# A transformer block on one core: the prologue in another order, the spline factors spread over attention periods, and all periods written out

## The chip, the core and the metric

One NeuronCore of a Trainium2 chip runs the whole program. The metric is the device time of one execution in microseconds (us). TensorE (PE) does matmuls and transposes, VectorE (DVE), ScalarE (ACT) and GpSimd (POOL) the rest; SyncE (SP) and, here also ScalarE, issue DMAs.

## What is computed

For x of 16 blocks of 256 tokens by 256 channels in float32, four residual steps follow one another (cut from the reference):

```python
x = x + attn_a(layernorm(x), Wq, Wk, Wv, Wo)        # 16 heads of 16, causal softmax
x = x + ffn(layernorm(x), gate_cp, up_cp, down_cp)
x = x + attn_b(layernorm(x), Wq, Wk, Wog, Wig, g_weight)  # gated linear attention, 16 keys
x = x + ffn(layernorm(x), gate_cp, up_cp, down_cp)

def ffn(h):
    gate_w, up_w, down_w = (spline_reconstruct(cp) for cp in ...)   # cubic, 2033 points to 1024 x 256
    return (silu(h @ gate_w.T) * (h @ up_w.T)) @ down_w.T
```

## The kernel before

Each engine has its own instruction list, written by hand; engines meet at semaphores only. The lists run through five stages: a prologue, the softmax attention, the first FFN, the gated attention (GLA), the second FFN.

Attention takes the 16 blocks one after the other in `period(b, j, u)`, with eight steps `p` (a step is a pair of heads from each half of the array). In step p TensorE computes for block b the scores with the row maxima subtracted (`shifted`, L878), for block b+1 the plain scores whose row maxima VectorE takes (`scores` L847, `hide_future` L859, `maxima` L1703), and every second step it weighs the values (`weigh`, L892 and L896). ScalarE takes the exponential (`exps`, L1322) and POOL zeroes what lies ahead of the diagonal (`mask`, L668). Between these stand the transposes and projections of block b+2 (`turn_x` L818, `proj_qk` with the three-matmul product `mm3` L414 to L416) and the end of block b-1 (`turn_o` L905, `turn_att` L913, `proj_out`). Q and K in high and low float parts are staged in `stage` (L1310, L1694) and moved by DMA into `stack` (L505), whose partitions hold the parts that one matmul contracts; six DMAs of 128 KB make one half of the stack (`stack_half`), two halves a block. Four small DMAs a half bring the maxima as rows (`max_rows`, L513). `run_periods` writes out periods 0, 1 and 12 to 15 and runs 2 to 11 as a loop of two.

The prologue, before period 0: SP loads the first X (L481), eight weights in a row on one semaphore (L483, L485), further X and the spline tables. VectorE sets constant rows of `stack` with four memsets (L1646) and then normalises block 0. TensorE waits for all eight weights, transposes them into `prep_bank` (L805, L809), ScalarE and VectorE split each in a high and a low part, and then come blocks 0 and 1 up to their stack rows, and the scores of block 0.

The weights of the FFN come from spline control points as low-rank factors. POOL makes them in `factors(w)` for gate, up and down (L678 product, L681, L683 and L686 sums) and `low_factors` (L690), before `rstd(2, 0)` and the first mask. In period 0 TensorE transposes the factors (`turn_factors` L934, one of four in each of steps 0 to 3; `turn_down` L945 in steps 6 and 7), ScalarE stores them (L1344, L1349). In period 1 `down_rows` (L959, K = 42) and `spread_rows` (L1360, L1362) make the down weight, which SP stores to DRAM at the end of period 1, together with two DMAs of zero rows.

Of the kernel before, what the change touches and what calls it, by code (L numbers as in the profile page):

```python
# [26 lines left out]
P = 128  # L27
B = 16
# [120 lines left out]
def build(nc, x, a_wq, a_wk, a_wv, a_wo, b_wq, b_wk, b_wog, b_wig, g_weight, cpw_in, psi_in, feat_in, mom_in,  # L149
          starts, out):  # L150
    outer = ExitStack()
    with outer:
# [14 lines left out]
        prep_bank = bank + [pair_a[:, 0], pair_a[:, 1], pair_b[:, 0], pair_b[:, 1]]  # L167
        fill_bank = prep_bank[2:] + prep_bank[0:2]
# [116 lines left out]
        s_w = sem("weights_loaded")  # L285
# [9 lines left out]
        s_stack = sem("stack_rows_set")  # L295
# [175 lines left out]

        def out_bank(u, q):

            return ((bank_o, bank_y)[q][:, :], pair_b[:, q, :])[1 - u]
# [5 lines left out]
        def _(sp):  # L480
            sp.dma_start(X[:, 0:TB, :], x_t[:, 0:TB, :]).then_inc(s_x[0], 16)  # L481
            for n, w in enumerate((a_wq, a_wk, a_wv, a_wo, b_wog, b_wig)):
                sp.dma_start(wnat[:, n], w.rearrange("(o p) c -> p o c", p=P)).then_inc(s_w, 16)  # L483
            for n, w in enumerate((b_wq, b_wk)):
                sp.dma_start(bnat[:, n, :], w).then_inc(s_w, 16)  # L485
            sp.dma_start(X[:, TB:2 * TB, :], x_t[:, TB:2 * TB, :]).then_inc(s_x[1], 16)
            sp.dma_start(cpw[:, :, :, :].rearrange("p w m k -> p (w m k)"), cpw_in).then_inc(s_cp, 16)
            sp.dma_start(flat[:, 14 * D:14 * D + MT * NF * WIN], psi_in).then_inc(s_cp, 16)
            sp.dma_start(X[:, 2 * TB:4 * TB, :], x_t[:, 2 * TB:4 * TB, :]).then_inc(s_x[2], 16)
            lead(sp, a_stk + a_md + f_.sp)  # L490
            sp.dma_start(mom[:, :, :], mom_in).then_inc(s_mom, 16)

            def stack_half(b, u, h, after_use=True):
# [4 lines left out]
                if after_use:  # L498
                    sp.wait_ge(a_stp, upto(a_stp, b - 2, 4 * h + 4))
                for a in range(2):  # L500
                    src = slice(HALF * a, HALF * a + HALF)
                    for r in range(3):
                        rows = slice(HALF * a + DK * r, HALF * a + DK * r + DK)
                        slots = slice(2 * r, 2 * r + 2) if r < 2 else slice(0, 4, 3)
                        sp.dma_start(stack[rows, u, h].bitcast(F32),  # L505
                                     stage[src, h, slots, :].bitcast(F32)).then_inc(a_stk[h], 16)

            def max_rows(b, u, h):
                sp.wait_ge(a_ml, upto(a_ml, b, h + 1))
                for a in range(2):  # L510
                    for n in range(2):
                        row = HALF * a + K_S + n
                        sp.dma_start(stack[row:row + 1, u, h, :, 0, :].bitcast(F32),  # L513
                                     mrow[PR * a:PR * a + PR, h, n, :].bitcast(F32)).then_inc(a_md[h], 16)

            for b in range(2):
                for h in range(2):
                    if not h:
                        sp.wait_ge(s_stack, 2 * b + 2)
                    if b and h:  # L520
                        max_rows(0, 0, 0)
                    stack_half(b, b, h, False)
            sp.wait_ge(s_c, 12)
            sp.dma_start(feat.rearrange("p r c -> p (r c)"), feat_in).then_inc(s_feat, 16)
# [12 lines left out]
            def period(b, j, u, prev=True, nxt=True, nxt2=True, nxt3=True):  # L537
                if not isinstance(b, int) or b < B - 4:
# [11 lines left out]
                if isinstance(b, int) and b == 1:  # L550
                    store_down()
                    sp.wait_ge(s_zero, 1)
                    for half in range(2):
                        sp.dma_start(copies[half, :, D, :].rearrange("v (p k) -> v p k", k=32),
                                     zeros[48 * half:48 * half + 48, :]).then_inc(s_zeros, 16)
# [83 lines left out]
        def _(pool):  # L639
# [3 lines left out]
                               pattern=[[-1, P]], channel_multiplier=1).then_inc(s_ident, 1)  # L643
            lead(pool, by_pool + f_.pool + g_.pool)
            pool.memset(causal_neg[:, :, :, :], 0.0).then_inc(s_const, 1)
            pool.memset(half_neg[:, :], -0.5).then_inc(s_const, 1)
            pool.memset(quarter[:, :], 0.25).then_inc(s_const, 1)
            pool.memset(V[:, :, :, :, DK:DK + 1], 1.0).then_inc(s_const, 1)
            pool.memset(V[:, :, :, :, DK + 1:32], 0.0).then_inc(s_const, 1)
            pool.wait_ge(s_const, 5)  # L650
            for n in range(2):
                i = pool.affine_select(out=causal_neg[:, n], in_=causal_neg[:, n], compare_op=ALU.is_ge,
                                       fill=NEG, base=HALF * n, pattern=[[-HALF, 2], [1, P]],
                                       channel_multiplier=-1)
            i.then_inc(s_const, 1)
            pool.wait_ge(s_ident, 2)
            pool.tensor_copy(ident16[:, :], ident[:, :]).then_inc(s_const, 1)
# [1423 lines left out]
```

## Time and profile before

| | us |
|---|---|
| median of three runs (lowest, highest) | 851.18 (848.19, 854.52) |
| the profiled execution, device time | 852.93 |
| its span, first to last instruction | 851.2 |
| mean granted TensorE clock | 0.962 |
| PE, DVE, ACT, POOL busy | 776.4, 629.5, 494.8, 237.0 |

The span lies 1.7 us under the device time. Busy times are sums over the span; a share says nothing of the stage that it falls in, so the readings below go by stages. L12 is line 12 of the kernel.

### The profile page before, as it was taken

The page shows a single profiled execution, that of the slowest core. Times are in us where ns is not written, and L with a number is a line of the kernel's source. Part 1 is how long each engine was busy: PE and PEld are TensorE (multiplying, and loading weights), DVE is VectorE, ACT ScalarE, POOL GpSimd, SP SyncE. Part 2 cuts the span into 40 slices and gives each one's busy share as a digit, 9 for nine tenths or more (in the row PEclk, how much of TensorE's full clock was granted, in tenths as well). Part 3 has the DMA queues.
Part 4 walks back from the last instruction along what each step waited for, and adds up shares of the span by engine and source line. Part 5 has one row for each costly group of instructions (what it writes and reads, how often), then busy time and mean ns, then how long its engine had stood idle before and what let it go on. Part 6 is the DMA issues. An engine that isn't in the chain of part 4 may idle for free.

```text
span 851.2 us, 19705 instructions
## 1 busy us (share of the span) xinstructions
PE 776.4 (91%) x6676; PEld 657.4 (77%) x6676; DVE 629.5 (74%) x1272; ACT 494.8 (58%) x967; POOL 237.0 (28%) x306
## 2 busy tenths in 40 slices
PE   3689999999999999977999989999998879999988
PEld 3567767777777777746988889888888758889887
DVE  7464777777777788836778777789989748887765
ACT  3135545455454555655666657588878746666653
POOL 2942222223232223321000010055656552000000
PEclk9767999999999999977999999999999989999999
DMA  5946566666666654577565651000034125777741
GB/s 183 112 69 88 94 124 100 88 88 88 98 98 94 96 80 78 109 248 262 204 230 218 255 204 45 1 2 2 2 111 168 42 79 202 255 259 272 267 159 50
DMA packets 70960, 111.16 MB, mean 131 GB/s; under 512 B 7061, under 2 KB 27958, under 8 KB 70854
## 3 DMA queue, kind: packets, MB, share of 16 engines
q1 hardware_dynamic: 70896, 110.35, 51.0%
q8 instruction: 35, 0.57, 0.3%
q14 instruction: 29, 0.24, 0.1%
HBM read 41.82 MB, written 42.81 MB: 99 GB/s over the span
## 4 chain that ended last, share of the span: by engine, by line
PE 51%; DVE 14%; issue 9%; DMA 8%; SPq 8%; ACT 6%; POOL 3%; ACTq 0%; DVEq 0%; POOLq 0%
PE bank L414 8%; PE bank L415 6%; PE bank L416 6%; DMA stk<-fx 5%; PE pair_a L878 4%; SPq L586 4%; PE bank L892 4%; PE pair_b L847 4%; DVE inter L1874 3%; DMA fx<-fs 3%; PE pair_a L1166 2%; ACT gact L1457 2%; DVE spline L1952 2%; PE bank L1201 2%; DVE spline L1961 1%
## 5 line engine op out<-in xcount | busy, mean ns | idle before, releaser
L414 PE MATMUL bank<-wd_hi,in_hi 128*128 128x256 f32 x512 | 145.5, 284 | 1.4 <-DVE in_lo L1879 0.9
L416 PE MATMUL bank<-wd_hi,in_lo 128*128 128x256 f32 x512 | 144.9, 283 | 0.0
L415 PE MATMUL bank<-wd_lo,in_hi 128*128 128x256 f32 x512 | 144.5, 282 | 0.0
L668 POOL TENSOR_SCALAR_AFFINE_SELECT prob<-prob 128x512 f32<-128x512 f32 x128 | 82.1, 642 | 217.3 <-ACT prob L1322 217.3
L1322 ACT ACTIVATE prob<-pair_a 128x768 f32<-128x768 f32 x128 | 103.7, 810 | 66.5 <-PE pair_a L878 65.5
L1465 ACT ACTIVATE in_hi<-inter 128x512 fp32r<-128x512 f32 x128 | 80.8, 631 | 105.7 <-DVE inter L1874 100.6
L1703 DVE TENSOR_REDUCE mx<-pair_b 128x6 f32<-128x768 f32 x124 | 118.0, 952 | 26.2 <-PE pair_b L859 25.3
L1879 DVE TENSOR_TENSOR in_lo<-inter,in_hi 128x512 fp32r<-128x512 f32 x128 | 89.1, 696 | 60.5 <-ACT in_hi L1465 59.0
L414 PEld LDWEIGHTS bank<-wd_hi,in_hi 128*128 128x128 f32 x512 | 96.7, 189 | 6.9 <-DVE in_lo L1879 1.7
L415 PEld LDWEIGHTS bank<-wd_lo,in_hi 128*128 128x128 f32 x512 | 96.5, 188 | 4.6
L416 PEld LDWEIGHTS bank<-wd_hi,in_lo 128*128 128x128 f32 x512 | 96.5, 189 | 0.0
L1874 DVE TENSOR_TENSOR inter<-gact,pair_b 128x512 f32<-128x512 f32 x128 | 87.1, 680 | 3.2 <-ACT gact L1457 2.2
L1457 ACT ACTIVATE gact<-pair_a 128x512 f32<-128x512 f32 x128 | 74.5, 582 | 3.3 <-PE pair_a L1111 3.3
L878 PE MATMUL pair_a<-stack 50*128 50x256 f32 x512 | 66.9, 339 | 10.2 <-ACT prob L1322 6.2
L878 PEld LDWEIGHTS pair_a<-stack 50*128 50x128 f32 x512 | 40.1, 191 | 36.1 <-issue 14.7
L847 PE MATMUL pair_b<-stack 48*128 48x256 f32 x496 | 57.0, 307 | 7.4 <-DVE stage L1694 3.7
L1111 PE MATMUL pair_a<-stk,cst 126*128 126x512 f32 x128 | 52.5, 410 | 9.4 <-DMA stk<-fx 8.1
L720 POOL TENSOR_TENSOR frs<-fve,half_neg 128x4 f32<-128x4 f32 x16 | 16.7, 1041 | 142.1 <-DVE fve L1853 142.1
L1114 PE MATMUL pair_b<-stk,cst 126*128 126x512 f32 x128 | 53.0, 414 | 1.7 <-DVE inter L1874 1.6
L1310 ACT ACTIVATE stage<-bank 128x512 fp32r<-128x512 f32 x32 | 19.2, 599 | 56.7 <-PE bank L416 52.0
L847 PEld LDWEIGHTS pair_b<-stack 48*128 48x128 f32 x496 | 40.0, 194 | 14.6 <-DVE mx L1703 7.6
L892 PE MATMUL bank<-prob,V 128*32 128x256 f32 x512 | 42.3, 403 | 0.3 <-POOL prob L668 0.2
(226 smaller groups left out, 1953.1 us busy)
## 6 DMA issues: line engine op xcount, KB each, us to landing
stk<-fx SPq DMA_DIRECT2D x128, 252.0 KB
stack<-stage SPq DMA_DIRECT2D x192, 128.0 KB, 4.7
fx<-fs SPq DMA_DIRECT2D x32, 512.0 KB, 3.4
fx<-fs SPq DMA_DIRECT2D x32, 256.0 KB, 3.6
fx<-fs SPq DMA_DIRECT2D x16, 504.0 KB
fx<-fs SPq DMA_DIRECT2D x16, 252.0 KB
X<-in_attn_a_x SPq DMA_DIRECT2D x14, 256.0 KB, 5.1
result<-X SPq DMA_DIRECT2D x7, 512.0 KB, 7.9
```

The costliest lines, as they stand in the source:

```text
L414: pe.matmul(dst, l_hi, r_hi, start=first, stop=False)
L415: pe.matmul(dst, l_hi, r_lo, start=False, stop=False)
L416: return pe.matmul(dst, l_lo, r_hi, start=False, stop=last)
L668: pool.affine_select(out=diag, in_=diag, compare_op=ALU.is_ge, fill=0.0, base=0, pattern=[[0, 2], [0, 2], [1, P]], channel_multiplier=-1). ...
L847: pe.matmul(dst[:, n, at_col:at_col + S], stack[rows, u, h, p % PR, 0, P * t:P * t + P], stack[rows, u, h, p % PR, 1, :], start=(t == 1), ...
L878: i = pe.matmul(pair_a[:, n, at_col:at_col + S], stack[rows, u, h, p % PR, 1, P * t:P * t + P], stack[rows, u, h, p % PR, 0, :], start=Tru ...
L1322: act.activation(prob[:, p % 4], pair_a[:, :, P:4 * P], ACT.Exp, scale=DK ** -0.5).then_inc(a_e, 1)
L1457: act.activation(gact[:, m % 2, :], pair_a[:, m % 2, :], ACT.Silu).then_inc(f_.si, 1)
L1465: act.activation(in_hi[:, m % LAG, :], inter[:, m % 2, :], ACT.Copy).then_inc(f_.ih, 1)
L1703: dve.tensor_reduce(mx[:, h, :, p % PR, :], src[:, :, 0:3 * P].rearrange("p n (t k) -> p n t k", t=3), AX.X, ALU.max).then_inc(a_mx, 1)
L1874: dve.tensor_tensor(inter[:, m % 2, :], gact[:, m % 2, :], pair_b[:, m % 2, :], ALU.mult).then_inc(f_.up, 1)
L1879: dve.tensor_tensor(in_lo[:, m % LAG, :], inter[:, m % 2, :], in_hi[:, m % LAG, :].bitcast(F32), ALU.subtract).then_inc(f_.il, 1)
```

## The change

1. Prologue. SP issues X of block 0, Wq, Wv, X of block 1, Wo, X of blocks 2 and 3; ScalarE issues Wk, Wog, Wig and the two small weights before its semaphore counts. Wq and Wk, and Wv, have semaphores of their own. VectorE keeps one memset of `stack` rows, POOL does the other three, and POOL's constants are ordered by need. TensorE takes the weights one by one, mixed with block 0 and 1; the second `proj_qk` of a block goes to another bank. Between them stand `keep_clock(n)`, n matmuls of 128 x 128 bf16 whose result nobody reads.
2. The spline tables are loaded behind the stack rows of blocks 0 and 1. Of each half, ScalarE issues the two DMAs of r = 2 and SP the four others.
3. The factors are 24 pieces on POOL (eight a weight), one behind each mask from step 4 of period 0 to step 3 of period 3; the low parts follow in steps 4 and 5 of period 3.
4. Two turns a period: `turn_factors` in periods 4 and 5, `turn_down` in 6, `down_rows` in 7 and 8, in steps 0 and 1, with two banks in turn. The store of the down weight follows period 8, the zero rows go one each to periods 1 and 2, the load of `feat` to period 3.
5. All periods are written out.
6. The DMAs of r < 2 name a row of 2 KB (`(k s)`) where they named two of 1 KB.

The core of the diff:

```diff
-            period(1, 0, 1)
-            with eng.Fori(1, B // 2 - 2) as j:
-                period(2 * j, j, 0)
-                period(2 * j + 1, j, 1)
-            period(B - 4, B // 2 - 2, 0)
+            for b in range(1, B - 3):
+                period(b, b // 2, b % 2)
...
+        def stack_rows(eng, u, h, r):
+            for a in range(2):
...
+                to, of = stack[rows, u, h].bitcast(F32), stage[src, h, slots, :].bitcast(F32)
+                if r < 2:
+                    to, of = to.rearrange("p i k s -> p i (k s)"), of.rearrange("p k s -> p (k s)")
+                eng.dma_start(to, of).then_inc(a_stk[h], 16)
...
             def period(b, j, u, prev=True, nxt=True, nxt2=True, nxt3=True):
                 for p in range(NP):
                     mask(b, p)
+                    if 4 <= NP * b + p < 28:
+                        factor_piece(NP * b + p - 4)
+                    if NP * b + p in (28, 29):
+                        low_factors(p - 4)
...
+            def keep_clock(n, dst=bank_y):
+                for _ in range(n):
+                    pe.matmul(dst[:, 0:P], ident16[:, :], ident16[:, :], start=True, stop=True)
...
+            pe.wait_ge(s_ident, 3)
+            keep_clock(40, pair_b[:, 1])
+            pe.wait_ge(s_wqk, 32)
+            turn_weight(0)
+            turn_weight(1)
+            turn_x(0, 0)
+            pe.wait_ge(s_wv, 16)
+            turn_weight(2)
+            keep_clock(8, pair_b[:, 1])
+            pe.wait_ge(s_prep_lo, 2)
+            pe.wait_ge(a_xl, upto(a_xl, 0, 1))
+            proj_qk(0, 0, 0)
+            proj_qk(0, 0, 1, bank_o)
+            pe.wait_ge(s_prep_lo, 3)
+            proj_v(0, 0)
+            turn_x(1, 1)
+            keep_clock(16, pair_b[:, 1])
+            turn_weight(3)
+            keep_clock(8, pair_b[:, 1])
+            pe.wait_ge(a_xl, upto(a_xl, 1, 1))
+            pe.wait_ge(a_qkl, upto(a_qkl, 0, 1))
+            proj_qk(1, 1, 0)
+            pe.wait_ge(s_const, 6)
+            pe.wait_ge(s_prep_lo, 4)
+            keep_clock(16)
+            for p in range(4):
+                hide_future(scores(0, 0, p, both=True))
+                if p == 1:
+                    keep_clock(8)
+            pe.wait_ge(a_qkl, upto(a_qkl, 0, 2))
+            proj_qk(1, 1, 1, bank_o)
+            turn_max(0, 0)
+            keep_clock(6)
+            for p in range(4, NP):
+                hide_future(scores(0, 0, p, both=True))
+                if p == 5:
+                    keep_clock(8)
+            for n in range(4, 6):
+                turn_weight(n)
+                keep_clock(16, bank_t)
...
+                    if 4 <= b < 9 and p < 2:
+                        if p == 0:
+                            pe.wait_ge(a_at, upto(a_at, b - 1, 1))
+                        else:
+                            pe.wait_ge(a_res, upto(a_res, b - 2, 1))
+                        if b < 6:
+                            turn_factors(2 * (b - 4) + p)
+                        elif b == 6:
+                            turn_down(p)
+                        else:
+                            down_rows(2 * (b - 7) + p)
+                    if 4 <= b < 9 and p in (2, 3):
+                        if b < 7:
+                            pe.wait_ge(s_ce, 2 * (b - 4) + p - 1)
+                        else:
+                            pe.wait_ge(s_wdn, 2 * (b - 7) + p - 1)
```

## Rows read from the trace of the kernel before

**Rows 1.** The page: TensorE's granted clock in tenths, 40 equal slices.

```profile
PEclk9767999999999999977999999999999989999999
```

**Rows 2.** Windows: start:end, length, busy us per engine, clock, DMA share, GB/s.

```profile
0.00:47.21 47.21, 23.96 (x170) 20.64 (x170) 29.48 (x54) 10.24 (x22) 29.76 (x31) 0.85 0.73 144
47.21:72.42 25.21, 22.48 (x220) 16.73 (x218) 15.75 (x35) 12.62 (x19) 7.07 (x11) 0.80 0.49 71
72.42:100.10 27.68, 27.36 (x263) 22.16 (x260) 15.68 (x33) 14.55 (x30) 6.05 (x9) 0.82 0.49 72
100.10:121.81 21.71, 19.68 (x234) 15.02 (x234) 15.86 (x34) 10.35 (x16) 5.81 (x9) 1.00 0.70 132
121.81:301.65 179.84, 175.12 (x2054) 134.19 (x2052) 139.16 (x289) 92.17 (x135) 52.34 (x81) 1.00 0.65 94
301.65:321.36 19.71, 19.26 (x232) 14.90 (x228) 15.53 (x33) 10.24 (x15) 5.82 (x9) 1.00 0.58 85
33.60:57.40 23.80, 18.16 (x130) 13.45 (x131) 15.59 (x27) 4.98 (x8) 16.13 (x14) 0.51 0.76 101
74.50:84.80 10.30, 10.30 (x71) 8.46 (x71) 2.74 (x4) 6.15 (x16) 1.28 (x2) 0.52 0.54 66
```

**Rows 3.** Timeline of the prologue: start us, length us, engine, line, out<-in [idle before, releaser].

```profile
2.37 1.28 ACT L1291 ACT_TABLE_LOAD   x1 [2.37 <-issue]
...
8.05 1.76 DVE L1646 MEMSET stack<- 32x2048 f32 x1 [0.48 <-issue]
...
9.84 0.75 DVE L1651 BATCH_NORM_STATS2 st<-X 128x6 f32<-128x256 f32 x2
...
10.49 3.64 PE L805 MATMUL bank<-ident,spline 128*128 128x128 f32 x16 [10.49 <-DMA spline<-in_attn_b_Wk]
...
18.39 0.39 PE L414 MATMUL bank<-xT_hi,wq_hi 128*128 128x256 f32 x1 [1.48 <-DVE xT_lo L1689]
...
21.77 14.19 SPq L505 DMA_DIRECT2D stack<-stage  x18
...
30.76 0.60 ACT L1310 ACTIVATE stage<-bank 128x512 fp32r<-128x512 f32 x1 [4.78 <-DMA stack<-stage]
...
32.13 0.50 PE L847 MATMUL pair_b<-stack 48*128 48x256 f32 x4 [3.69 <-DVE stage L1694]
...
33.68 0.95 DVE L1703 TENSOR_REDUCE mx<-pair_a 128x6 f32<-128x768 f32 x1
...
47.21 0.81 ACT L1322 ACTIVATE prob<-pair_a 128x768 f32<-128x768 f32 x1 [4.69 <-PE pair_a L878]
```

**Rows 4.** Timeline of POOL's factor work and the transpose behind it.

```profile
21.15 4.25 POOL L678 TENSOR_TENSOR spline<-spline,cpw 128x2016 f32<-128x2016 f32 x1 [3.23 <-DVE xn L1663]
...
28.38 1.09 POOL L686 TENSOR_TENSOR cx<-spline 128x336 f32<-128x336 f32 x1
...
47.76 0.71 PEld L934 LDWEIGHTS bank<-ident,cx 128*126 128x126 f32 x4 [0.20 <-POOL cx L690]
```

**Rows 5.** Timeline of one middle period: second mask, its weighing, four transposes.

```profile
184.47 0.64 POOL L668 TENSOR_SCALAR_AFFINE_SELECT prob<-prob 128x512 f32<-128x512 f32 x1 [1.07 <-ACT prob L1322]
...
185.48 0.64 PE L892 MATMUL bank<-prob,V 128*32 128x256 f32 x8
...
186.76 0.60 PE L905 MATMUL bank<-ident,oT 128*128 128x128 f32 x4
...
187.29 0.50 PE L878 MATMUL pair_a<-stack 50*128 50x256 f32 x4
```

**Rows 6.** Timeline of the down rows in period 1: matmuls and their ScalarE copies.

```profile
77.52 2.87 PE L959 MATMUL bank<-spline 42*128 42x128 f32 x12
...
79.58 0.84 ACT L1360 ACTIVATE spline<-bank 128x192 f32<-128x192 f32 x2 [0.76 <-PE bank L959]
...
80.22 0.36 ACT L1362 ACTIVATE spline<-bank 128x128 f32<-128x128 f32 x1
```

**Rows 7.** DMA totals of two stretches: 24 to 34 us, then 168 to 188 us.

```profile
DMA packets 962, 1.26 MB, mean 126 GB/s; under 512 B 151, under 2 KB 546, under 8 KB 962
...
q1 hardware_dynamic: 962, 1.26, 109.2%
...
DMA packets 1564, 1.88 MB, mean 94 GB/s; under 512 B 240, under 2 KB 1052, under 8 KB 1564
```

More of the change, by code:

```diff
@@ L497, in stack_half @@
                 sp.sem_inc(passed_sp, 1)
[L498 to L506, printed above, removed]
+                sp.wait_ge(a_stp, upto(a_stp, b - 2, 4 * h + 4))
+                for r in range(3):
+                    stack_rows(sp, u, h, r)
             def max_rows(b, u, h):
@@ L549, in period @@
                     stack_half(b + 2, u, 1)
-                if isinstance(b, int) and b == 1:
+                if b in (1, 2):
+                    sp.wait_ge(s_zero, 1)
+                    sp.dma_start(copies[b - 1, :, D, :].rearrange("v (p k) -> v p k", k=32),
+                                 zeros[48 * (b - 1):48 * b, :]).then_inc(s_zeros, 16)
+                if b == 3:
+                    sp.wait_ge(s_c, 24)
+                    sp.dma_start(feat.rearrange("p r c -> p (r c)"), feat_in).then_inc(s_feat, 16)
+                if b == 8:
                     store_down()
[L552 to L555, printed above, removed]
                 if nxt and not nxt2:
@@ L643, in _, with ones_rows @@
                                pattern=[[-1, P]], channel_multiplier=1).then_inc(s_ident, 1)
+            pool.wait_ge(s_ident, 2)
+            pool.tensor_copy(ident16[:, :], ident[:, :]).then_inc(s_ident, 1)
+            pool.memset(half_neg[:, :], -0.5).then_inc(s_const, 1)
             lead(pool, by_pool + f_.pool + g_.pool)
[L645 to L657, printed above, removed]
-            pool.memset(zeros[:, :], 0.0).then_inc(s_zero, 1)
+            def ones_rows(u, a):
+                rows = slice(HALF * a + 2 * DK, HALF * a + HALF)
+                pool.memset(stack[rows, u, :, :, 1].bitcast(F32), 1.0).then_inc(s_stack, 1)
+                pool.wait_ge(s_stack, 2 * u + a)
             def rstd(b, u):
@@ L691, in low_factors @@
                                    ALU.subtract).then_inc(s_c, 1)
+            pool.wait_ge(s_const, 1)
+            ones_rows(0, 1)
             rstd(0, 0)
+            pool.memset(quarter[:, :], 0.25).then_inc(s_const, 1)
+            pool.memset(V[:, :, :, :, DK:DK + 1], 1.0).then_inc(s_const, 1)
+            pool.memset(V[:, :, :, :, DK + 1:32], 0.0).then_inc(s_const, 1)
             rstd(1, 1)
-            pool.wait_ge(a_xn, upto(a_xn, 1, 2))
-            for w in range(3):
-                factors(w)
-            for w in range(2):
-                low_factors(w)
+            pool.memset(causal_neg[:, :, :, :], 0.0).then_inc(s_const, 1)
+            pool.wait_ge(s_const, 5)
+            for n in range(2):
+                i = pool.affine_select(out=causal_neg[:, n], in_=causal_neg[:, n], compare_op=ALU.is_ge,
+                                       fill=NEG, base=HALF * n, pattern=[[-HALF, 2], [1, P]],
+                                       channel_multiplier=-1)
+            i.then_inc(s_const, 1)
+            pool.wait_ge(s_const, 6)
+            ones_rows(1, 0)
+            ones_rows(1, 1)
             rstd(2, 0)
-            pool.wait_ge(s_prep_lo, 7)
+            pool.memset(zeros[:, :], 0.0).then_inc(s_zero, 1)
             def period(b, j, u, prev=True, nxt=True, nxt2=True, nxt3=True):
@@ L1641, in _ @@
         def _(dve):
-            for u in range(2):
-                for a in range(2):
-                    rows = slice(HALF * a + 2 * DK, HALF * a + HALF)
-                    dve.memset(stack[rows, u, :, :, 1].bitcast(F32), 1.0).then_inc(s_stack, 1)
+            dve.memset(stack[2 * DK:HALF, 0, :, :, 1].bitcast(F32), 1.0).then_inc(s_ones, 1)
             lead(dve, by_dve + f_.dve + g_.dve)
@@ L1777, in period @@
                         maxima(b + 1, p)
+                        if b == 0 and p == 1:
+                            low_gla_weights()
                         if p == 3:
```

334 lines of the change are left out of this document (172 added, 162 removed).

## The prediction

> **What bounds the kernel now.** I read four views in this order. The page's clock line [rows 1] first: TensorE is granted less than its full clock in two places, at the start and near slices 18 and 19. Then the windows from the first exponential of one attention period to the next [rows 2], which give the length of each piece of the attention stage; the reader should see that nine periods in the middle take 179.84 us (19.98 each) with TensorE busy 175.12 us at clock 1.00, so they are bound by TensorE, while the prologue takes 47.21 us with TensorE busy 23.96, and the first three periods take 25.21, 27.68 and 21.71 us. Against a middle period that is 14.9 us too much in the three. Third, the timeline of the prologue [rows 3] and its POOL and TensorE rows [rows 4], to see what arrives late. Fourth, the timeline of one middle period [rows 5], because the work that leaves the prologue goes there.
>
> The prologue is a queue of late starts. VectorE sets constant rows until 9.81 us and only then reads the first X [rows 3]. TensorE waits for the last of eight weight loads and starts its transposes at 10.49. The first projection runs at 18.39, the first stack loads are issued at 21.77, the copy of the next projection waits for them until 30.76, and the first scores run at 32.13. From there to the first exponential at 47.21 are 15.1 us, of which the eight row maxima take 8 x 0.95; the clock is 0.51 in 33.6 to 57.4 [rows 2]. Beside that chain POOL makes the spline factors from 21.15 on, and TensorE's first factor transpose, at 47.76, waits for the last of them [rows 4]. So two chains end within a microsecond, and taking away the POOL one alone would give little.
>
> **The change, part by part.** The sum is made against the profiled execution, 852.93 us, which lies 1.75 above the median of 851.18.
>
> *Earlier start of the prologue.* Three of the four VectorE memsets go to POOL or behind other work, so the statistics need only X and one memset (1.76 us from about 1.3, then some 1 to 2 us of semaphore counts): about 4 us instead of 9.84. The weights are issued on two queues, and TensorE waits for Wq and Wk alone. ScalarE now issues five loads ahead of its semaphore counts and table load, which began at 2.37 and take 1.28 [rows 3]; at some 0.5 us an issue it is ready at about 6.5. Then one weight eviction pair, xn, its transpose, and the two halves of xT give the first projection at about 9.8 (18.39 before, 8.6 earlier). From projection to stack issue stays 3.4, so the stack loads begin at about 13.
>
> *Stack loads.* A half of the stack is six loads of 128 KB. In 24 to 34 us the DMA engines are full at 1.26 MB in 10 us [rows 7], which makes 6.2 us a half. First issue to the wait's end was 9.0 us. Two of six issues go to ScalarE, some 1.3 us less of serial issue on SP, so I take 7.8 us: half 0 lands at about 20.9, and half 1, behind it, by 26. The rearranged rows of r < 2 ask for 2 KB pieces, but a middle period's 1564 packets hold 512 of 2 KB or more [rows 7], which is exactly eight loads of 64: these rows are 2 KB already. I cost that edit at nothing. Were they 1 KB after all, the two thirds of each half that they carry could at most move in half their time, 2 us off the wait for a half; the other bound is 0. The Trainium skill, "DMA: Bandwidth & Descriptors", section "Issuing engines are not separate DMA queues", says that issuing from several engines saves only the issue time, because all share 16 engines; by it the ScalarE issues give the 1.3 us and no more, whereas a second stream of its own would land half 0 some 3 us sooner. The full share in [rows 7] sides with the rule.
>
> *From the first scores to period 0.* Scores start at 20.9. VectorE then has eight maxima (7.6) and the evictions, merges and splits between them: of the 15.1 us before, 7.5 were not maxima, and I take 4.2 for these at full clock, together 11.8, with the wait for half 1 inside. TensorE has, after its last scores, two weight transposes (0.53 per four at full clock, [rows 5]; twice that cold) and 32 filler matmuls, 2 to 4 us. I take 13.6 us to the first exponential, 15.1 before, so 34.5. Gain 12.7 us. Bounds: 9 (the path from 32.13 is as long as before and the clock low) to 17 (the tail of weight transposes hidden).
>
> *Periods 0 to 2.* Factor and down-row work leaves them, and the clock, if kept, is 1.00. Period 0: a middle period less the part of the previous block (output projection, three groups of four transposes, a weighing), 17.5 us, gain 7.7. Period 1: 20.1, gain 7.6. Period 2: 20.0, gain 1.7; it was long because SP issued the 1 MB store and the zero rows between stack loads and max rows (its DMA rate is 132 GB/s against 94). Zero rows stay in 1 and 2, half each: at most 0.5 us each.
>
> *Written-out periods.* The one written-out period with the same work takes 19.71 [rows 2], the looped ones 19.98. Nine of them: minus 2.4 us. Lower bound of the gain 0, if the difference belongs to what is late in that period.
>
> *POOL pieces.* The factor work, 8.3 us a weight (21.15 to 29.47), is cut in eight pieces of at most 1.09 us ([rows 4]: 4.25 over four, and 1.09), one behind each mask in slots 4 to 27. What is queued behind a piece on POOL is the next mask, and behind that the weighing on TensorE. In a middle period the second mask starts at 184.47 and ends at 185.11; its weighing starts at 185.48 [rows 5]. The mask before ends 1.07 us ahead of it ([rows 5], the idle time). A piece makes the second mask at most 0.2 late, against a slack of 0.37. Cost 0, up to 0.4 a period for three periods. POOL also waits for the factor tables, which SP now issues behind all stack rows of both blocks, at about 33; with 1.2 MB behind the last half they land at about 42, and the piece comes at about 43. No wait, or up to 3 us if both err.
>
> *Turns in periods 4 to 8.* These periods are TensorE-bound, so this lies on the path. Six groups of four transposes at 0.53 [rows 5] make 3.2 us. The down rows are 32 matmuls, twelve of them in 2.87 us at clock 0.5 [rows 6], 0.22 each with what overlaps, so 0.11 at clock 1.00: 3.5 us (bound 7.0). ScalarE sits between them: a store is an eviction of 0.60, as the copy in [rows 3], and down rows are 0.84 + 0.36 [rows 6], and it stands between two exponentials, for which TensorE's next step waits. I take 0.5 us of stall in the three lighter periods and 1.0 in the two heavier ones, 3.5 in all (bounds 0 and the whole ScalarE work, 9). The 1 MB store now follows period 8: 1.2 us, as period 2 shows its like. Together 11.3.
>
> *Rest.* FFN and GLA stages are the same. Sum: -12.7 - 7.7 - 7.6 - 1.7 - 2.4 + 11.3 = -20.8, so 832.1 for the profiled execution and 830.4 by the median.
>
> **The rivals.** (a) The clock is lost as before, after the prologue and once more in periods 4 to 8. It fell at 33.6, after TensorE had stood idle for 3.69 us ahead of the first scores [rows 3], and again in 74.5 to 84.8, while the down rows ran [rows 2]. A stretch of 10.3 us at half clock can cost TensorE-bound work 5.1 us and work that waits for others nothing; I take 4.5, since the middle periods are TensorE-bound. Two of them: 839. For: maxima on VectorE pace TensorE at less than half busy. Against: fillers stand at those gaps. The Trainium skill, "TensorE: Matmul & The Clock Gate", Part 4, says that transposes do not count as activity for the clock; a prologue full of transposes would then start cold. The trace has 16 transposes from 10.49 [rows 3] and no loss behind them: a mean of 0.85 over the prologue [rows 2] is what half clock from 33.6 alone gives; I give the rule part of this rival's chance, and its cost here would be the transposes at twice their time, some 3 us. (b) The added turns are absorbed by TensorE's small gaps and ScalarE never stalls, and the tail of the prologue is hidden: 830.4 - 3.5 - 4 = 823. (c) Slower side: masks become the bound. If each piece came ahead of a mask that TensorE waits for, all 24 pieces and the two low parts, at 1.06 on average ([rows 4]: 4.25 over four), would be on the path, 27.5 us, and the time 858. It decides once a piece, mask and handover exceed the 1.71 us between the first masks by more than 0.37, in every slot; the mean spacing of masks is 19.98 / 8 = 2.5 us, which speaks against it. (d) The new order does not start sooner because X, Wq and Wk land late beside other loads and ScalarE's table load comes last: the first projection at 14 instead of 9.8, result 835.
>
> **How the numbers follow.** My forecast has 0.55, (a) 0.18, (b) 0.12, (d) 0.12, (c) 0.03. The likeliest gives 830.5. The range 821 to 841 takes in (a), (b) and (d) with the bounds of the stall and the prologue tail. About 1% (8.5 us) is what a measurement of this kernel can tell from no change; only (c), or a sum of (a) and (d) with another lost stretch, reaches that: faster by over 1% 0.93, within 1% 0.05, slower 0.02.
>
> **What would show it.** First projection at about 10, first scores at 21, first exponential at 34 to 35; period 0 near 17.5; periods 1 to 3 near 20 with clock 1.00; periods 4 to 6 at 21.2 and 7 and 8 at 22.5; unchanged packets of 2 KB a period; weighings that never name POOL as releaser. It would be wrong if the clock is low after 35 us, if scores wait for half 1 well after 26, or if the middle periods with pieces are longer than those without.

## The result, and the profile after

The changed kernel takes 841.9 us (median of 20 runs, 836.74 to 848.79) where the kernel before takes 850.63 (20 runs, 844.65 to 857.96): a ratio of 0.991, 95% interval 0.989 to 0.993. That is 8.7 us less, where 20.7 were forecast, and it lies just outside the forecast range of 821 to 841. The profiled execution took 838.48 us, its span is 836.7, and its mean granted clock 0.975.

The page's clock line first. A stretch in which TensorE is granted half its clock is called a lost stretch below. The low slices of [rows 1] near the start are gone but for one.

```profile
PEclk9899999999999999978999999999999999999999
```

The windows of the changed kernel, as in [rows 2]: the prologue, periods 0, 1 and 2, the nine periods 3 to 11, the six periods 4 to 9, period 8 alone, and all behind the last block's first exponential.

```profile
0.00:39.39 39.39, 29.24 (x308) 26.59 (x308) 23.73 (x47) 8.62 (x14) 10.92 (x21) 0.91 0.72 144
39.39:59.33 19.94, 16.58 (x200) 12.52 (x196) 15.45 (x38) 9.83 (x18) 10.24 (x13) 1.00 0.64 131
59.33:79.35 20.02, 19.45 (x230) 14.75 (x226) 16.37 (x34) 10.87 (x18) 14.78 (x18) 1.00 0.67 99
79.35:99.27 19.92, 19.50 (x232) 15.16 (x232) 16.39 (x33) 10.61 (x16) 14.07 (x17) 1.00 0.56 92
99.27:288.09 188.82, 179.96 (x2112) 140.51 (x2108) 140.45 (x291) 98.83 (x154) 57.75 (x88) 0.99 0.63 98
119.39:248.39 129.00, 122.04 (x1428) 95.83 (x1424) 93.04 (x193) 68.01 (x109) 34.75 (x54) 0.99 0.63 100
204.06:226.87 22.81, 22.25 (x248) 17.53 (x244) 15.34 (x32) 12.07 (x23) 5.79 (x9) 0.93 0.57 79
346.04:836.70 490.66, 451.33 (x3084) 405.68 (x3082) 366.55 (x730) 320.51 (x695) 117.42 (x137) 0.97 0.43 155
```

Against the profiled execution of before, stage by stage from the first exponentials:

| stage | forecast | measured |
|---|---|---|
| prologue | -12.7 | 39.39 - 47.21 = -7.8 |
| period 0 | -7.7 | 19.94 - 25.21 = -5.3 |
| period 1 | -7.6 | 20.02 - 27.68 = -7.7 |
| period 2 | -1.7 | 19.92 - 21.71 = -1.8 |
| periods 3 to 11 | -2.4 + 11.3 = +8.9 | 188.82 - 179.84 = +9.0 |
| all behind | 0 | -0.9 |
| sum | -20.8 | -14.5 |

The likeliest value forecast for the median was 830.5, and 841.9 was measured, 11.4 more (the remaining 0.6 of the 12.0 is the kernel before, whose median was 851.18 in three runs and 850.63 in twenty). Of these 11.4 us, 6.4 stand in this table, in its first two lines; the other 5.0 lie between the profiled execution and the median.

The prologue, as in [rows 3].

```profile
11.05 0.36 PE L416 MATMUL bank<-xT_hi,wq_hi 128*128 128x256 f32 x1 [0.94 <-DVE xT_lo L1770]
...
13.38 1.37 ACTq L484 DMA_DIRECT2D stack<-stage  x2
...
13.58 1.15 DVE L1744 TENSOR_SCALAR xn<-X,mv,rs 128x256 f32<-128x256 f32 x2 [0.82 <-POOL rs L676]
...
14.65 1.47 DVE L1775 TENSOR_TENSOR stage<-bank,stage 128x512 fp32r<-128x512 f32 x2
...
15.43 0.73 SPq L484 DMA_DIRECT2D stack<-stage  x1
...
24.68 0.80 PE L891 MATMUL pair_b<-stack 48*128 48x256 f32 x4 [3.42 <-DMA stack<-stage]
...
39.39 0.81 ACT L1384 ACTIVATE prob<-pair_a 128x768 f32<-128x768 f32 x1 [0.73 <-PE pair_a L922]
```

The first projection came at 11.05 (18.39 before). ScalarE issued its two loads at 13.38, but the low part, from which SP's four are made, stood on VectorE behind the normalising of block 1 and was done only for an issue at 15.43. The half landed for scores at 24.68, 9.3 us after SP's first issue and 11.3 after ScalarE's, with the DMA engines full: 18 to 28 us moved

```profile
DMA packets 871, 1.21 MB, mean 121 GB/s; under 512 B 145, under 2 KB 414, under 8 KB 871
```

against 1.26 MB in ten microseconds in [rows 7]. From there to the first exponential are 14.7 us, 15.1 before. This execution was a quick one here: in nine profiled executions with this prologue (seven of them with a change further on) the first exponential stands at 39.39 to 42.25 us, and 39.39 is the earliest.

The chain of work that ends period 0 (start, us, what):

```profile
53.91 0.23 PE bank L910 x2
54.16 0.42 DVE mrow L1797
54.61 0.42 DVE mrow L1799
55.05 0.67 SPq L489
55.76 0.65 SPq L489
56.45 0.57 SPq L489
57.06 1.69 DMA stack<-mrow
58.79 0.50 PE pair_a L922 x4
```

The reader should see the queue: the max of block 1 is transposed, split in two, issued by SP in four DMAs one after the other, and carried in 1.69 us; only then can TensorE start period 1. It stood 1.62 us for it, of 3.4 in all in a period in which it was busy 16.58 us; the other stops are under 0.6 each. In a middle period the same chain takes as long, 262.84 to 267.9, but the work of the block before fills the time. This is read from the trace; no run shortens the chain.

The timeline of period 4, then of period 9.

```profile
121.13 0.60 ACT L1406 ACTIVATE cst<-bank 126x512 fp32r<-126x512 f32 x1 [0.93 <-PE bank L974]
...
121.79 1.64 SPq L573 DMA_DIRECT2D spline<-down_features  x1
...
122.10 0.82 ACT L1384 ACTIVATE prob<-pair_a 128x768 f32<-128x768 f32 x1
...
123.94 1.34 SPq L489 DMA_DIRECT2D stack<-mrow  x2
...
130.12 0.50 PE L922 MATMUL pair_a<-stack 50*128 50x256 f32 x4 [1.34 <-DMA stack<-mrow]
...
229.27 0.61 SPq L544 DMA_DIRECT2D wdx<-spline  x1
...
231.07 3.15 SPq L489 DMA_DIRECT2D stack<-mrow  x4
...
237.26 0.50 PE L922 MATMUL pair_a<-stack 50*128 50x256 f32 x4 [1.78 <-DMA stack<-mrow]
```

The feature loads and the 1 MB store stand on SP ahead of the max rows, which are issued behind them and land late: TensorE stops 1.34 and 1.78 us in front of the second half of the block.

### The profile page after: what moved, and what is told of

Same layout as the page of the kernel before. It is cut to its first block, busy times and chain, and to the rows that moved or that the text cites. A ratio compares the mean times of both kernels' runs of the same rounds, so it can differ in the third digit from the quotient of the medians.

```text
span 836.7 us, 19306 instructions
## 1 busy us (share of the span) xinstructions
PE 772.9 (92%) x6818; PEld 658.4 (79%) x6818; DVE 626.0 (75%) x1269; ACT 493.8 (59%) x967; POOL 243.5 (29%) x321
## 2 busy tenths in 40 slices
DMA packets 70983, 111.48 MB, mean 133 GB/s; under 512 B 7061, under 2 KB 27958, under 8 KB 70854
## 4 chain that ended last, share of the span: by engine, by line
PE 54%; DVE 14%; issue 9%; SPq 8%; DMA 8%; ACT 7%; ACTq 0%; DVEq 0%; POOL 0%; POOLq 0%
PE bank L416 9%; PE bank L418 8%; PE bank L417 8%; PE pair_a L922 4%; DMA stk<-fx 4%; PE bank L936 3%; DVE inter L1961 3%; PE pair_b L891 3%; SPq L606 3%; SPq L489 3%; PE pair_a L1222 2%; PE pair_a L1167 2%; DMA stack<-mrow 2%; PE pair_b L1170 2%; DVE spline L2039 2%
## 5 line engine op out<-in xcount | busy, mean ns | idle before, releaser
L1784 DVE TENSOR_REDUCE mx<-pair_b 128x6 f32<-128x768 f32 x124 | 118.0, 951 | 35.0 <-PE pair_b L903 34.6
L417 PEld LDWEIGHTS bank<-wd_lo,in_hi 128*128 128x128 f32 x512 | 98.2, 192 | 4.8
L418 PEld LDWEIGHTS bank<-wd_hi,in_lo 128*128 128x128 f32 x512 | 98.2, 192 | 0.0
L922 PEld LDWEIGHTS pair_a<-stack 50*128 50x128 f32 x512 | 39.3, 188 | 39.6 <-DMA stack<-mrow 13.4
L891 PE MATMUL pair_b<-stack 48*128 48x256 f32 x496 | 54.6, 296 | 4.7 <-DMA stack<-stage 3.4
L1170 PE MATMUL pair_b<-stk,cst 126*128 126x512 f32 x128 | 54.9, 429 | 1.7 <-DVE inter L1961 1.6
```

Source lines behind the costliest of these rows:

```text
L417: pe.matmul(dst, l_hi, r_lo, start=False, stop=False)
L418: return pe.matmul(dst, l_lo, r_hi, start=False, stop=last)
L891: pe.matmul(dst[:, n, at_col:at_col + S], stack[rows, u, h, p % PR, 0, P * t:P * t + P], stack[rows, u, h, p % PR, 1, :], start=(t == 1), ...
L922: i = pe.matmul(pair_a[:, n, at_col:at_col + S], stack[rows, u, h, p % PR, 1, P * t:P * t + P], stack[rows, u, h, p % PR, 0, :], start=Tru ...
L1784: dve.tensor_reduce(mx[:, h, :, p % PR, :], src[:, :, 0:3 * P].rearrange("p n (t k) -> p n t k", t=3), AX.X, ALU.max).then_inc(a_mx, 1)
```

## The experiments

Unless said otherwise each changes the changed kernel. "Six periods" are 4 to 9, which hold all the moved turns and the store. The kernel before, run beside them, took 848.89 (first four), 850.38 (next four) and 851.09 us (last four).

**Before, written out.** The loop of before is replaced by its periods; nothing else.

```diff
-            with eng.Fori(1, B // 2 - 2) as j:
-                period(2 * j, j, 0)
-                period(2 * j + 1, j, 1)
+            for b in range(1, B - 3):
+                period(b, b // 2, b % 2)
```

> The kernel before with its ten looped attention periods written out, nothing else. Theory A (the loop costs 0.27 us a period, as the one written-out period of the same work showed): 2.7 us faster, ratio 0.997, each period 19.7. Theory B (the 0.27 belongs to what that one period leaves out; written-out code gives nothing back or has to be fetched): ratio 1.000 or above, periods at 20.0 or more. Theory B, if true, would account for part of the gain that is missing from the median.

Measured 846.49 us (12 runs), ratio 0.996 (0.993 to 0.999). Windows of period 1 and of the nine:

```profile
71.25:94.18 22.93, 22.61 (x262) 18.28 (x259) 15.56 (x33) 14.10 (x30) 6.06 (x9) 1.00 0.58 88
115.61:294.29 178.68, 173.28 (x2056) 134.05 (x2052) 138.68 (x289) 92.42 (x136) 52.34 (x81) 1.00 0.64 96
```

Five of the nine periods are 19.65, the others up to 20.60, and the nine are 1.2 us shorter than in [rows 2], the medians 2.4: the theory that the loop costs something stands, with 1 to 3 us. The row of period 1 says more. The work is that of before, with the down rows in it, and it takes 22.93 us at full clock where the profile of before has 27.68 at 0.82 [rows 2]. So 4.8 of the 7.6 us that I expected from period 1 belonged to a lost stretch, which the same work need not have.

**Turns twice.** TensorE's added matmuls of periods 4 to 8 are issued twice, ScalarE's copies once.

```diff
-                for k in range(4):
+                for k in (0, 1, 2, 3) * 2:
```

(the same in the three turn functions)

> The changed kernel with each group of factor transposes and down-row matmuls on TensorE done twice over. Theory A (this work lies on the path at full clock in periods 4 to 8): 6.7 us more than the changed kernel, ratio to the kernel before 0.999, periods 4 to 6 up by 1.1 and 7 and 8 by 1.8. Theory B (what makes periods 4 to 8 long is ScalarE's copies and the loads in between, TensorE has room): under 2 us more, ratio 0.992 to 0.993.

Measured 843.12 us (12 runs), ratio 0.992 (0.989 to 0.996). The window of the six periods, and behind it that of the next kernel, whose six periods are those of the changed kernel without the stretch of half clock in its period 8:

```profile
119.45:250.49 131.04, 126.34 (x1484) 101.02 (x1480) 93.06 (x193) 68.64 (x109) 34.88 (x54) 1.00 0.59 98
```

```profile
37.88:62.03 24.15, 20.66 (x200) 15.58 (x196) 16.83 (x40) 10.05 (x19) 10.32 (x13) 0.78 0.57 116
123.36:250.95 127.59, 120.52 (x1428) 94.90 (x1424) 93.06 (x193) 68.03 (x109) 34.74 (x54) 1.00 0.65 101
```

56 matmuls more cost 131.04 - 127.59 = 3.5 us, not the 6.7 that I had charged for the first 56. TensorE has some room there, but the work is not free. By the medians the two kernels cannot be told apart.

**No fillers.** The matmuls that are there only for the clock are left out.

```diff
-                for _ in range(n):
+                for _ in range(0):
                     pe.matmul(dst[:, 0:P], ident16[:, :], ident16[:, :], start=True, stop=True)
```

> The changed kernel without the 126 filler matmuls of the prologue. Theory A (they keep the clock up): clock low from about 24 us for 10 to 24 us, prologue and period 0 together 3 to 6 us longer, ratio to before 0.995 to 0.998. Theory B (the clock follows the idle stretch of 3.4 us before the first scores, which no filler covers, and TensorE is not the bound of the prologue): the same low stretch as with them, prologue shorter by the 3 us that the fillers take near its end, ratio 0.988 to 0.991.

Measured 844.58 us (12 runs), ratio 0.994 (0.991 to 0.997). The first exponential is 1.5 us earlier (37.88), and period 0 is 4.2 longer at clock 0.78 (above), period 1 1.3 longer. By the ratios the fillers earn 2.4 us, with intervals that overlap. That they keep the clock in periods 0 and 1 is not shown: five profiles with these fillers have a lost stretch there too, one of them 23.00 us at 0.78 in period 0 (both moves, below).

**One queue.** All six loads of a half, and the max rows, are issued by SP.

```diff
-                    for r in range(2):
+                    for r in range(3):
                         stack_rows(sp, b, h, r)
```

(with ScalarE's issues left out)

> The changed kernel with all stack and maximum rows of the prologue issued by SP, none by ScalarE. Theory A (the DMA engines are full from the first stack load on, so the queue that issues does not matter): first scores within 1 us of the 24.7 of the changed kernel, ratio to before 0.990 to 0.993. Theory B (issue time of 0.65 us each on SP sets the landing): first scores 1.3 to 2.6 us later, and again before period 0, ratio 0.994 to 0.996.

Measured 842.71 us (8 runs), ratio 0.990 (0.987 to 0.994), not to be told from the changed kernel.

```profile
16.46 7.81 SPq L484 DMA_DIRECT2D stack<-stage  x12
...
25.39 0.80 PE L889 MATMUL pair_b<-stack 48*128 48x256 f32 x4 [4.15 <-DMA stack<-stage]
```

The first scores come 0.7 us later than with two queues, but in this execution the first projection was 1.0 us later as well (12.08 against 11.05). From the first projection to the first scores are 13.3 us with one queue and 13.6 with two, so the 1.3 us of issue time that I had taken off were not to be had. The windows from the first issue to the landing, two queues and then one, show what else was moved:

```profile
13.38:24.68 11.30, 7.23 (x80) 6.67 (x78) 4.90 (x11) 2.29 (x4) 5.84 (x8) 0.98 0.85 116
```

```profile
16.46:25.39 8.93, 4.78 (x64) 4.54 (x62) 2.95 (x8) 1.68 (x3) 3.99 (x4) 0.88 0.88 117
```

The rate is the same. When half 0 had landed, 11.30 x 116 = 1.31 MB had moved with two queues and 8.93 x 117 = 1.04 MB with one, and half 0 is 0.79 MB of either. The loads of half 1 do not wait behind half 0, and ScalarE's two of them, issued at 15.43 beside SP's first, are the extra quarter of a megabyte.

**Stores behind the max rows.** Zero rows, feature loads and the 1 MB store are issued after the period's max rows.

```diff
                 max_rows(b, u, 1)
+                if b in (1, 2):
+                    sp.wait_ge(s_zero, 1)
...
+                if b == 4:
+                    sp.wait_ge(s_c, 24)
...
+                if b == 8:
+                    store_down()
                 if nxt2:
                     stack_half(b + 2, u, 0)
```

> The changed kernel with SP's large extra DMAs (zero rows in periods 1 and 2, the 336 KB of features, the 1 MB store) issued behind the first four maximum rows of a period, where the DMA engines are idle, instead of behind the last stack rows of a period. Theory A (they delay the maximum rows of the next period, for which TensorE waited 1.34 us in period 4): period 4 shorter by 1.2, period 9 by 1.5, periods 2 and 3 by 0.1, 3 us in all, ratio to before 0.987 to 0.988. Theory B (the DMA engines are short of time as a whole, and the delay only moves to the stack rows behind): periods 4, 8 and 9 together the same within 1 us, ratio 0.991.

Measured 836.12 us (5 runs, 834.42 to 838.66), ratio 0.984 (0.980 to 0.988).

```profile
119.89:243.95 124.06, 120.35 (x1428) 94.92 (x1424) 92.89 (x193) 67.85 (x109) 34.74 (x54) 1.00 0.65 104
```

The six periods lose 4.9 us against the changed kernel, or 3.5 against the one without a lost stretch: periods 4 and 9 fall from 21.88 to 20.58 and from 21.52 to 19.67, and both stops of TensorE are gone. Of the avoidable costs that were tried, this order was the largest.

**Later copies.** ScalarE's copies of the turned factors are put one step later.

```diff
-                    if 4 <= b < 9 and p < 2:
+                    if 4 <= b < 9 and 1 <= p < 3:
...
-                            store_factors(2 * (b - 4) + p)
+                            store_factors(2 * (b - 4) + p - 1)
```

> The changed kernel with ScalarE's copies of the turned factors and down rows one step later in its list, behind the next exponential, in periods 4 to 8. Theory A (periods 4 to 8 are long because the copy stands ahead of the next exponential, which TensorE waits for; doing TensorE's part twice cost only 2 us of 6.7): periods 4 to 8 shorter by 0.5 to 1 us each, 3 to 4 us in all, ratio to before 0.986 to 0.988. Theory B (TensorE's own added work sets the length): unchanged within 0.3 us a period, ratio 0.991.

Measured 838.8 us (5 runs), ratio 0.986 (0.982 to 0.990).

```profile
60.43:83.71 23.28, 23.13 (x230) 17.03 (x228) 15.69 (x33) 10.99 (x17) 14.58 (x17) 0.80 0.57 82
123.76:249.37 125.61, 120.42 (x1428) 95.08 (x1424) 92.82 (x193) 68.88 (x110) 34.88 (x54) 1.00 0.65 102
```

2.0 us less than 127.59 in the six periods: in the changed kernel the copy at 121.13 stood ahead of the exponential at 122.10. Periods 4 and 9, where TensorE stops for the max rows, stay at 21.8 and 21.5. Its period 1 shows the lost clock that the profile of the changed kernel has not, with the same program up to there.

**Whole factor operations.** 12 POOL operations of full size in place of the 24 pieces, in every second slot.

```diff
-                m = slice(2 * k, 2 * k + 2)
-                pool.tensor_tensor(prod[:, m], psi[:, m], ...
+                pool.tensor_tensor(prod, psi, ...
...
-                    if 4 <= NP * b + p < 28:
+                    if 4 <= NP * b + p < 28 and p % 2 == 0:
```

> The changed kernel with the factor work on POOL in 12 whole operations (4.25, 1.91, 0.8 and 1.1 us) behind every second mask of the same four periods, instead of 24 pieces of at most 1.1 us. Theory A (a late mask holds up the weighing on TensorE, and small pieces are what avoids it): each 4.25 us operation holds one mask up by about 2 us, periods 0 to 2 longer by 1 to 2.5 us each, ratio to before 0.994 to 0.998. Theory B (the weighing comes late enough, or the clock and VectorE hide it): within 0.5 us a period, ratio 0.991, and then the pieces of the change earn nothing over whole operations.

Measured 845.39 us (10 runs), ratio 0.994 (0.991 to 0.996), by the ratios 2.0 us more than with pieces. Period 2 is 21.23 us at full clock (19.92 in pieces). The timeline there:

```profile
97.60 4.24 POOL L694 TENSOR_TENSOR spline<-spline,cpw 128x2016 f32<-128x2016 f32 x1
...
98.92 2.94 DVE L1736 TENSOR_SCALAR ve<-mv 128x2 f32<-128x2 f32 x1
...
101.77 0.95 DVE L1782 TENSOR_REDUCE mx<-pair_b 128x6 f32<-128x768 f32 x1
...
102.77 0.50 PE L889 MATMUL pair_b<-stack 48*128 48x256 f32 x4 [1.06 <-DVE mx L1782]
```

I had expected late masks, and they are late. But the stop of TensorE names VectorE: an operation on 128x2 elements, 0.17 us elsewhere, lasts until POOL's product ends, and the maximum behind it is late by that. So the size came as expected, and part of the mechanism is another.

**Early low part.** Both moves, and the low part of block 0 ahead of the normalising of block 1.

```diff
-            normalise(1, 1)
             low_qk(0, 0)
+            normalise(1, 1)
```

> The changed kernel with both edits above, the large DMAs in the gap and the copies one step later, and VectorE's low part of the first projection ahead of the normalisation of block 1 in the prologue. Theory A for both: 6 us from them, and stack loads issued 1.1 us sooner, first exponential near 38.5 instead of 39.4; ratio to before 0.982 to 0.985. If only one of them holds: 0.986 to 0.988. Theory B for both: 0.990 to 0.991.

Measured 834.98 us (5 runs), ratio 0.982 (0.978 to 0.985).

```profile
15.37 5.44 SPq L484 DMA_DIRECT2D stack<-stage  x8
...
26.04 0.51 PE L891 MATMUL pair_b<-stack 48*128 48x256 f32 x4 [3.60 <-DMA stack<-stage]
```

In this execution X reached the transposed form 1.2 us later (11.41 against 10.22), so from there SP's issue is 1.3 us sooner, but the half took 10.7 us from it to land. From the first projection (12.24) to the first scores are 13.8 us, against 13.6 in the changed kernel, so the earlier issue buys nothing that can be seen. The first exponential came at 42.55, not at the 38.5 expected: a second lost stretch of 3.4 us, from 37.3, is in that time.

**Once more.** The changed kernel unchanged, profiled again.

> The changed kernel as it is, profiled a second time beside the next three kernels. Theory C (the profile of after that the prediction is held against was a quick execution, and typical ones lose the clock once more in periods 0 and 1): the profile shows either periods 0 and 1 of 19.9 to 20.1 us as before, or one of them at 22 to 23.5 us with a stretch of half clock of 3 to 10 us; median 840 to 843 on this chip. Rival (the clock never falls there in this kernel and the median lies above the profile for another reason, FFN and GLA stages): no stretch of half clock between 35 and 100 us, and the rest after the last block more than 2 us longer than the 490.7 of the first profile.

Measured 841.89 us (6 runs), ratio 0.989 (0.985 to 0.994); this profiled execution took 841.99, the median itself.

```profile
346.50:840.30 493.80, 451.95 (x3084) 406.25 (x3082) 366.87 (x730) 320.39 (x695) 117.52 (x137) 0.97 0.43 154
```

The attention stage agrees within 0.5 us, period by period within 0.12. The rest is 3.1 us longer. So the rival holds for this pair: it is in the FFN and GLA stages, which the change does not touch, that this typical execution is longer than the first one. Cut into four stretches of the same work, the rest takes 130.96, 24.00, 185.00 and 150.70 us in the first execution at clock 0.93, 0.93, 0.99 and 0.98, and 132.00, 25.85, 185.95 and 150.00 in the second at 0.94, 0.87, 0.98 and 0.99. The last three together, 2.1 us, go with the clock; the first, 1.0, does not.

**Fillers before period 1.** 24 filler matmuls where TensorE stands for the max rows, first alone, then with the two moves; between them, the two moves without them.

```diff
+                    if b == 0 and p == 7:
+                        pe.wait_ge(a_ml, upto(a_ml, 1, 1))
+                        keep_clock(24, bank_t)
```

> The changed kernel with 24 filler matmuls at the end of period 0, where TensorE stands 1.62 us for the DMA of the first max rows of block 1. Theory C (the clock is lost in periods 0 and 1 of typical executions because of that stop): no half clock between 35 and 100 us, median 1.5 to 3 us below the changed kernel of the same call. Rival (the loss there comes from the sparse work of period 0 as a whole, or doesn't explain the median): median within 1 us of the changed kernel.

Measured 840.87 us (6 runs), ratio 0.988 (0.984 to 0.993): 1.0 below the changed kernel run beside it, and a stretch of 3.4 us at half clock in period 0 all the same.

> The two moves that gained apart (stores and feature loads issued behind the max rows of the period; ScalarE's copies one step later) together, without the early low part. If their gains add: 4.7 us from the stores and 1.5 to 3 from the copies, 834 to 836 where the changed kernel has 841. If they are the same stall seen twice: 836 to 838, no better than the stores alone.

Measured 837.41 us (6 runs), ratio 0.984 (0.980 to 0.988).

```profile
40.65:63.65 23.00, 20.62 (x200) 15.50 (x196) 15.64 (x38) 10.05 (x19) 10.26 (x13) 0.78 0.55 113
124.76:247.62 122.86, 120.28 (x1428) 95.12 (x1424) 92.65 (x193) 68.62 (x109) 34.74 (x54) 1.00 0.66 105
```

> The kernel before this one with the 24 filler matmuls at the end of period 0 as well. Theory C: 1.5 to 3 us below it, 832 to 834. Rival: the same within 1 us.

Measured 832.8 us (6 runs, 830.47 to 836.46), ratio 0.979 (0.975 to 0.984), the best of all.

```profile
42.25:62.19 19.94, 18.02 (x224) 13.86 (x220) 15.45 (x38) 9.84 (x18) 10.28 (x13) 1.00 0.55 121
...
122.26:244.83 122.57, 120.26 (x1428) 95.09 (x1424) 92.64 (x193) 68.67 (x109) 34.88 (x54) 1.00 0.64 105
```

In the six periods the gains of the two moves nearly add: 127.59 to 124.06 by the one (3.5), to 125.61 by the other (2.0), to 122.6 to 122.9 by both (4.7 to 5.0). In the medians they don't show as a sum (0.984 with both, 0.984 with the stores alone); the profile with both moves and no fillers shows lost clock in periods 0 and 1 (23.00 us at 0.78), which may be the reason and is not shown for the other runs. What the fillers before period 1 are worth stays open: 1.0 us alone, 4.6 on top of the two moves (intervals that overlap), 1.8 by the ratios against the kernel with both moves and the early low part, and period 0 has the same 19.94 us with and without them, when the clock holds.

## Why the prediction was wrong

Three steps failed, of 4.9, 2.4 and 5.0 us. The time lies outside the range by 0.9, so with any one of the three right it would have been inside.

*Prologue, -12.7 forecast, -7.8 measured.* "The first projection at about 9.8" came at 11.05, 1.2 late. The stack loads, forecast to begin at "about 13", began at 13.4 on ScalarE and 15.4 on SP, where two operations of block 1 stand on VectorE ahead of the low part. The step that failed is the landing: "I take 7.8 us: half 0 lands at about 20.9, and half 1, behind it". It landed at 24.68, 11.3 us after the first issue. The 6.2 us a half of which the 7.8 are made want the DMA engines for half 0 alone, and the 1.31 MB moved by then show that half 1 shared them. Neither one queue (13.3 us from the first projection) nor SP's issue 1.3 us sooner (13.8) changes the 13.6 by more than 0.3. "13.6 us to the first exponential" was 14.7, with the clock at 0.53 from 24.6 to 31.4, behind TensorE's stop of 3.42 before the first scores; what that clock cost was not tried. Together 4.9.

*Period 0, 17.5 forecast, 19.94 measured.* The step took away TensorE's work of the previous block and let the rest shrink by as much. TensorE's busy time did fall, to 16.58; the period is then ended by the max rows' chain, and I named no rival of that kind. TensorE's stop at its end is 1.6 of the 2.4 us; the rest is spread over shorter stops.

*Periods 1 to 3.* 20.1 and 20.0 forecast, 20.02, 19.92 and 20.12 measured, clock 1.00. Right.

*Turns and written-out periods, +8.9 forecast, +9.0 measured.* The sum is right by luck, for its terms are not. Against six quiet written-out periods (6 x 19.66 = 118.0) the changed kernel's 129.0 hold about 4.6 for TensorE's added work (what is left when both moves are made, 122.6, so it can hold other things too; doing the work twice added 3.5; I had 6.7), 1.2 to 2.0 for ScalarE's copies (3.5), 2.8 to 3.5 for loads and store ahead of the max rows (1.2, and for the store alone), and 1.4 for a stretch at half clock in period 8. Such a stretch, of 3.4 us in period 8 or 9, is in five of the eight profiles with the store ahead of the max rows and in none of the four with it behind; that this order keeps the clock is a likely reading and not shown. The two heavy periods were forecast at 22.5 and took 21.77 and 22.81; period 9 at 21.52 was not in the forecast at all.

*POOL pieces at nothing.* Held: TensorE never waits for a mask of POOL by more than 0.2 us in periods 0 to 3, though the longest pieces took 1.2 us and not "at most 1.09". *2 KB rows at nothing.* Held: the pages of both kernels count the same 7061, 27958 and 70854 packets under 512 B, 2 KB and 8 KB.

*From the profile to the median.* The third step is "the sum is made against the profiled execution, which lies 1.75 above the median", and that was all that was taken off, as if the profiled execution of after would lie above its median too. It lies 3.4 below; 1.6 off (832.1 to 830.5) and 3.4 on are the 5.0. (That of before lies 2.3 above the median of its 20 runs, so the table's 14.5 us are 5.7 more than the medians' 8.7.) How far a single execution lies from its median is partly a matter of luck.

The record of each run has its granted clock, and span x (1 - clock) x 2 is its time at half clock: 52 us in the median run of the changed kernel, 42 in the profiled one. Over the 20 runs the time follows it with 0.36 us for each microsecond (correlation 0.93), which makes 3.6 us. For the kernel before, 31 runs give 0.28 (0.89). This is a correlation, and it does not carry over to each pair of runs: the second profiled execution has 44 us by the same measure (the record has three digits of the clock, so each is right within 1 us) and took 841.99, 3.5 us more than the first, where the slope gives 0.7. Some 2.1 of them go with the clock stretch by stretch (above), and the others stay open. That the 3.4 us are mostly clock is likely and not shown.

The first experiment shows what the table hides: a lost stretch in period 1 of before counted for 4.8 us of the gain, though the same work runs without it in another execution. The changed kernel can lose clock there too: five other profiled executions have the same program through period 0, and two of them have a lost stretch in period 0 or 1. The rest of the program, the same in all 14 profiles, varies from 488.5 to 494.3 us.

Rival (a), the clock lost again twice, 839, is the nearest of my cases, and (d), a late start, 835, was partly true as well; (a) had its price about right for a period bound by TensorE (4.5 us for 10.3 forecast, 1.4 for 3.4 measured in period 8); what the lost stretch in the prologue cost is not known. In (d) the first projection was to be 4.2 us late, and it was 1.2.

## What to carry to other kernels

Split a profiled gain into what the work costs and what a lost stretch of clock cost in that one execution; the second part is to be priced by how often it occurs, from the clock of every run, not from one profile. When work is taken out of a period that is bound by one engine, follow the next chain to the period's end before you book the gain: here four serial DMA issues of max rows. Large stores and loads that nobody awaits go behind the small DMAs that the next step awaits, in the same queue; that alone was worth 3.5 to 4.9 us by the windows and 6 of 842 by the ratios. When a transfer is awaited, see what else is in flight before it lands: two queues did not bring the awaited half sooner, since they also brought its neighbour.

## What the hardware showed

*VectorE stands still while POOL works, for some operations.* POOL's piece, VectorE's copy beside it, and the same copy with POOL idle:

```profile
58.35 1.20 POOL L695 TENSOR_TENSOR spline<-spline,cpw 128x504 f32<-128x504 f32 x1
...
58.75 0.83 DVE L1791 COPY mx<-mx 128x8 f32<-128x8 f32 x1
...
267.75 0.17 DVE L1791 COPY mx<-mx 128x8 f32<-128x8 f32 x1
```

The copy ends with the piece, at 59.6. The maxima, which read PSUM, keep their 0.95 us beside POOL. The Trainium skill, "SBUF — State Buffer", section "SBUF: two separate sides", says that VectorE and GpSimd share a pair of ports as an exclusive lock. A VectorE operation in a two-port mode, or with two SBUF inputs, and a GpSimd operation exclude one another: the one that starts first holds the pair for its whole instruction and the other fully blocks. The 2.94 us of the experiment with whole operations and the 0.83 here agree with it; in which mode an operation ran no trace shows. I had priced a piece only by the mask behind it; shorter pieces also bound this stall. VectorE is busy 16.4 us in periods 1 and 2 against 15.5 in later ones; what of the 0.3 us by which these periods exceed 19.66 is due to it was not tried.

*The clock.* In every profile it fell to its lower level, half, during TensorE's stop before the first scores or within 1.2 us behind it (24.2 us in the changed kernel, 33.2 in the one before), with fillers and without. The six groups of transposes and the 32 down matmuls, doubled, did not lose it: 1.00 over the six periods.
